# A graph attention kernel: later x groups transposed between the matmuls of v, and the order of its prologue

## The reference

```python
h = jnp.maximum(_layernorm(x, axis=-1), 0.0)          # x: (4096, 256), eps 1e-5
q = h @ Wq.T + bq;  k = h @ Wk.T + bk;  v = h @ Wv.T + bv
a = q @ k.T / sqrt(256) + adj + adj                   # adj: (4096, 4096), added twice
out = x + jax.nn.softmax(a, axis=-1) @ v
```

## Time and profile before

| | before |
|---|---|
| time, median of 3 runs | 810.15 us (810.07 to 2887.47) |
| time of the profiled execution | 809.79 us |
| its span | 808.0 us |
| TensorE busy | 799.6 us, 99% |
| DVE busy | 561.3 us, 69% |
| GpSimd busy | 412.7 us, 51% |
| ACT busy | 357.2 us, 44% |

### The profile page before, as it was taken

The page is one execution under the profiler, slowest core; times in us unless marked ns, Lnnn a source line. Parts: engine busy times, 40 slices in busy tenths (PEclk is TensorE's granted clock), DMA queues, the critical chain, the costliest instruction groups (busy, mean ns, idle before and its releaser), DMA issues.

```text
span 808.0 us, 16606 instructions
## 1 busy us (share of the span) xinstructions
PE 799.6 (99%) x6652; PEld 797.6 (99%) x6652; DVE 561.3 (69%) x942; ACT 357.2 (44%) x637; POOL 412.7 (51%) x377
## 2 busy tenths in 40 slices
PE   9999999999999999999999999999999999999998
PEld 8999999999999999999999999999999999999998
DVE  6868767676676767667677666767766676776754
ACT  5684434434443443444344444344444444443365
POOL 4545719073471917447091643709164380926573
PEclk9999999999999999999999999999999999999999
DMA  8520434333333334333333333423333343333300
GB/s 256 180 94 5 161 91 120 98 112 97 97 114 93 112 98 110 100 98 119 92 111 93 112 105 91 123 92 106 101 111 106 83 123 91 110 105 94 91 27 14
DMA packets 46398, 83.57 MB, mean 103 GB/s; under 512 B 5616, under 2 KB 8304, under 8 KB 46320
## 3 DMA queue, kind: packets, MB, share of 16 engines
q1 hardware_dynamic: 45744, 81.71, 33.5%
q10 hardware_dynamic: 576, 0.79, 0.3%
HBM read 78.25 MB, written 4.23 MB: 102 GB/s over the span
## 4 chain that ended last, share of the span: by engine, by line
PE 95%; DVE 1%; ACT 1%; POOL 1%; issue 1%; DMA 0%; SPq 0%; POOLq 0%; DVEq 0%
PE ps L393 48%; PE ps L495 15%; PE ps L496 15%; PE ps L497 15%; PE ps L385 1%; PE ps L374 1%; DMA ring_b<-in_adj 0%; ACT x_pair L573 0%; PE ps L404 0%; POOL v L329 0%; DVE x_third L680 0%; POOL rstd L315 0%; SPq L234 0%; DVE ring_b L703 0%; ACT v_full L593 0%
## 5 line engine op out<-in xcount | busy, mean ns | idle before, releaser
L393 PE MATMUL ps<-qhl,hT 128*128 128x256 f32 x3072 | 407.2, 282 | 0.6 <-DVE ring_b L703 0.6
L393 PEld LDWEIGHTS ps<-qhl,hT 128*128 128x128 f32 x3072 | 383.9, 190 | 0.8 <-DVE ring_b L703 0.8
L495 PE MATMUL ps<-v,p_hi 128*128 128x258 f32 x1024 | 290.0, 283 | 0.3 <-DVE p_lo L744 0.3
L496 PE MATMUL ps<-v,p_lo 128*128 128x258 f32 x1024 | 288.8, 282 | 0.0
L497 PE MATMUL ps<-v,p_hi 128*128 128x256 f32 x1024 | 288.4, 282 | 0.0
L640 ACT CAST p_hi<-ps 128x512 fp32r<-128x512 f32 x256 | 150.3, 587 | 264.4 <-PE ps L497 262.6
L364 POOL TENSOR_TENSOR ring_a<-ring_a,m_row 128x512 f32<-128x512 f32 x179 | 226.0, 1300 | 16.3 <-ACT m_row L646 15.6
L703 DVE TENSOR_TENSOR ring_a<-ps,ring_a 128x512 f32<-128x512 f32 x179 | 123.3, 689 | 117.3 <-PE ps L393 116.4
L495 PEld LDWEIGHTS ps<-v,p_hi 128*128 128x128 f32 x1024 | 194.7, 190 | 0.5 <-DVE p_lo L744 0.5
L496 PEld LDWEIGHTS ps<-v,p_lo 128*128 128x128 f32 x1024 | 193.8, 189 | 0.0
L497 PEld LDWEIGHTS ps<-v,p_hi 128*128 128x128 f32 x1024 | 193.2, 189 | 0.0
(11 more groups left out here) (82 smaller groups left out, 340.0 us busy)
## 6 DMA issues: line engine op xcount, KB each, us to landing
ring_a<-in_adj SPq DMA_DIRECT2D x179, 256.0 KB, 2.7
ring_b<-in_adj SPq DMA_DIRECT2D x77, 256.0 KB, 2.7
x_res<-in_x SPq DMA_DIRECT2D x16, 256.0 KB, 3.0
out<-x_res SPq DMA_DIRECT2D x15, 256.0 KB, 2.0
x_pair<-in_x SPq DMA_DIRECT2D x5, 512.0 KB, 4.2
term_row<-term_spill SPq DMA_DIRECT2D x14, 128.0 KB, 3.2
x_third<-in_x SPq DMA_DIRECT2D x2, 512.0 KB, 4.3
w_all<-in_w ACTq DMA_DIRECT2D x3, 256.0 KB, 4.3
```

Source lines behind the costliest of these rows:

```text
L393: last = nc.tensor.matmul(dst, lhs(a, ib), rhs(c, ib), start=(n == 0), stop=(n == 3 * DB - 1))
L495: nc.tensor.matmul(ps[:, at, 0:VW], hi, v[:, n, 0:VW], start=(n == 0), stop=False)
L496: nc.tensor.matmul(ps[:, at, 0:VW], lo, v[:, n, 0:VW], start=False, stop=False)
```

## The change

TensorE's iteration of group g, for g from 1 to 6, no longer begins with the 8 transposes of group g + 1. A new function issues v's first half of group g, 12 matmuls, and puts one transpose behind each of the matmuls 3 to 10 (counted from 0), so that four matmuls stand ahead of the first transpose; the waits for the normalized rows and for the free PSUM banks stand between matmul 3 and the first transpose. It is one stream: transposes write to two banks of their own, and the sums of v run on between them. Block 1's q is computed in the last group, directly behind v's first half and ahead of scores(14); the wait for its low part before v's second half is gone, and the next that asks for it is scores(16). The order of ACT's, GpSimd's and SP's lists is unchanged but for `q_hi(1)`, which follows `Q1_GROUP` to group 7. On DVE the statistics of group g + 3 and their aggregation now stand directly behind `add_adj(2g - 1)`, both ahead of `h_lo`, and `h_lo` ahead of `running_max(2g - 1)`; `q_lo(1)` follows to group 7.

```diff
--- before.py
+++ after.py
@@ -24,7 +24,7 @@
     LAG = UNITS + 6
     HOLD = (STEPS - 5,)
     WARM = 20
-    Q1_GROUP = 3
+    Q1_GROUP = GROUPS - 1
     SPLIT_PARTS = 4
     PARTS = GROUPS + 1
     XB = 3
@@ -447,6 +447,27 @@
                                          lambda c, ib: wv_T[:, c, ib, :])
                 last.then_inc(s_vmm, 1)
 
+            def project_v_and_transpose_h(g):
+                pe.wait_ge(s_vhi, 2 * (g - 1) + 1)
+                for n in range(2):
+                    t = GT * g + n
+                    for i, (ib, a, c) in enumerate((ib, a, c) for ib in range(DB) for a, c in ((0, 0), (1, 0), (0, 1))):
+                        m = 3 * DB * n + i
+                        last = nc.tensor.matmul(ps[:, v_bank(g, 0) + n, 0:VW], hT[:, a, ib, t * P:(t + 1) * P],
+                                                wv_T[:, c, ib, :], start=(i == 0), stop=(i == 3 * DB - 1))
+                        if m == 3:
+                            if g + 2 < SPLIT_PARTS:
+                                pe.wait_ge(s_norm2, g + 2)
+                            pe.wait_ge(s_norm, g + 2)
+                            pe.wait_ge(s_hlo, g + 2)
+                        if 3 <= m < 3 + DB * GT:
+                            jb, j = (m - 3) // GT, (m - 3) % GT
+                            turned = nc.tensor.transpose(ps[:, HT_BANK + jb, j * P:(j + 1) * P],
+                                                         rows(g + 1)[:, j, jb * P:(jb + 1) * P], ident[:, :])
+                            if j == GT - 1:
+                                turned.then_inc(s_ht, 1)
+                last.then_inc(s_vmm, 1)
+
             def scores(s):
                 b, u = s // UNITS, s % UNITS
                 if u == 0:
@@ -516,18 +537,16 @@
             project_v(0, 1)
             scores(1)
             for g in range(1, GROUPS):
+                pe.wait_ge(s_hlo, g + 2)
                 if g + 1 < GROUPS:
-                    transpose_h(g + 2)
-                pe.wait_ge(s_hlo, g + 2)
-                project_v(g, 0)
-                scores(2 * g)
+                    project_v_and_transpose_h(g)
+                else:
+                    project_v(g, 0)
                 if g == Q1_GROUP:
                     pe.wait_ge(s_vhi, 2 * g)
                     project_q(1)
-                    scores(2 * g + 1)
-                    pe.wait_ge(s_qlo, 2)
-                    project_v(g, 1)
-                elif g + 1 < GROUPS:
+                scores(2 * g)
+                if g + 1 < GROUPS:
                     project_v(g, 1)
                     scores(2 * g + 1)
             scores(FIRST - 1)
@@ -803,15 +822,14 @@
                 tile_stats(3, j)
             part_stats(4)
             for g in range(1, GROUPS):
-                if g + 1 < GROUPS:
-                    h_lo(g + 2)
                 add_adj(2 * g - 1)
                 if g + XB < GROUPS:
                     for j in range(GT):
                         tile_stats(g + XB, j)
+                    part_stats(g + XB + 1)
+                if g + 1 < GROUPS:
+                    h_lo(g + 2)
                 running_max(2 * g - 1)
-                if g + XB < GROUPS:
-                    part_stats(g + XB + 1)
                 if g == Q1_GROUP:
                     q_lo(1)
                 add_adj(2 * g)
```

## The result

| | before | after |
|---|---|---|
| time, median of 22 runs each | 810.08 us | 808.41 us |
| ratio of the times | | 0.9983, 95% interval 0.9977 to 0.9989 |
| time and span of the profiled execution | 809.79, 808.0 us | 807.8, 806.0 us |
| scores(1)'s first matmul to the turn of block 0's maxima | 53.02 us | 51.50 us |

The change gives 1.67 us, 0.2% (by the interval 0.9 to 1.9 us); 808.5 us was forecast.

What follows compares the result with a forecast made beforehand. TensorE, 99% busy, bounds the kernel, with 3.2 us of lost time at most to recover. Terms of -0.48, -0.69, -0.59 and +0.1 us give -1.65 us: 808.5 us forecast, own range 807.9 to 809.1 us, overall 807.3 to 810.8 us.

Steps and rivals of the forecast that it cites:

- The sum: Whole change: -0.48 - 0.69 - 0.59 = -1.76 us, and +0.1 us for alternation, gives -1.65 us.
- the turn: Sign of being right: the turn of the maxima comes 1.6 to 1.8 us sooner than 71.38 us.
- Wait for x group 2: Group 1: v's first four matmuls fill part of TensorE's wait for DVE's normalization, -0.48 us.
- q's wait: Group 3: moving block 1's q to the last group removes the wait for its low part, -0.69 us.
- the 0.3 us of spare time: Last group: unit 14's logits are added 3.99 us from q's start; scores(16) needs them at 4.3 us.
- The chain behind group 3: Two groups behind group 3: a late start, hardly won back, goes with q's move; 0.64 us less 0.05 us.
- Alternation: Six groups, 48 transposes between matmuls: cost 0 to 0.2 us, taken as +0.1 us.
- the uncovered loads: Rival: weight loads uncovered at each switch between transpose and matmul, 8.2 us less 1.7 us gained, 816.6 us; chance 7%.
- the cheaper matmuls: Rival: a matmul beside a transpose is 0.01 us cheaper, 0.5 us in all, 808.0 us; chance 9%.
- What becomes later: Within groups: ACT's high part of h at 2.39 us, low part 3.45 us, normalizations end 6.6 to 6.7 us; covered.
- The statistics ahead of the low part of h: DVE's list: the move uses time DVE waited for ACT; without it adds are late, not TensorE; 0 us either way.
- The clock: Rival: thinned matmuls lower TensorE's clock to 1.2 GHz, groups 1 to 6 take twice 39.7 us, 849 us; chance 1%.

Runs made afterwards that it cites:

- e1_q_last: Kernel before with only block 1's q moved to the last group, transposes in blocks and DVE's order kept: 808.28 us, 0.9981 of before.
- e3_q_stays: Changed kernel with block 1's q put back into group 3 behind scores(6), with its wait: 808.86 us, 0.9987 of before.
- e11: Kernel before with DVE's new order alone, statistics and aggregation ahead of the low part of h: 809.59 us, 0.9994 of before.
- e4_block_behind_four: Changed kernel with a group's eight transposes in one block behind v's fourth matmul, without alternation: 808.00 us, 0.9978 of before.
- e5b_old_dve_order: Changed kernel with DVE's order of before (low part of h, add, statistics), second series: 809.93 us, 0.9995 of before.
- e8: Changed kernel with both halves of v ahead of eight transposes, ACT and DVE lists adapted, and two adj loads ahead of SP's second spill: 810.04 us, 1.0003 of before.
- e9: Changed kernel, v's halves ahead of transposes, adj loads ahead of second spill, low part of h before DVE's maximum and statistics in groups 1-2: 806.02 us, 0.9950 of before.
- e6: Changed kernel with both halves of v (24 matmuls) ahead of a block of eight transposes, ACT and DVE lists adapted: 810.27 us, 1.0007 of before.
- e7: Changed kernel with the last two adj buffers' first loads ahead of the second spill of score terms on SP: 807.05 us, 0.9966 of before.
- e2: Kernel before with block 1's q still in group 3 but ahead of scores(6): 809.54 us, 0.9997 of before.
- e5: Changed kernel with DVE's order of before (low part of h, add, statistics), first series: 809.97 us, 1.0002 of before.
- e10: Changed kernel, adj loads ahead of SP's second spill, v's first half ahead of eight transposes, DVE's statistics last in the group: 806.42 us, 0.9957 of before.

## Why the prediction was right

The sum was -1.65 us; the medians give -1.67 us and the stretch -1.52 us. That the first two agree to 0.02 us is luck: the interval reaches from 0.9 to 1.9 us, and the turn came 2.0 us sooner, outside the 1.6 to 1.8 us forecast, because 0.48 us of it lie ahead of the change. The mechanism is borne out by the traces, term by term, from the starts of matmuls:

- *Wait for x group 2:* 0.48 us forecast, 0.39 us found (from the last matmul ahead to the first transpose 2.03 us before, 1.64 us after). DVE's normalization ended 0.1 us later against scores(1) than before, having taken 2.41 us instead of 2.33 us.
- *q's wait:* 0.69 us, all of it, shown by e1_q_last. q's low part was written 3.4 us and the add behind it 3.97 us from q's start (62.19 to 66.16 us), 3.99 us having been forecast: the 0.3 us of spare time were real.
- *The chain behind group 3:* 0.59 us, gone. The step named moving q as what removes it, and e1_q_last shows that this is enough. But the rest of the change removes it as well (e3_q_stays), which the prediction said only of slack in general and did not weigh, and 0.35 us of it go with DVE's new order alone (e11). Its reason was only half read: in the second group it was not a late start that is hardly won back, but one GpSimd operation that took 0.74 us in place of 0.20 us beside DVE's running maximum.
- *Alternation:* 0.1 us taken from 0 to 0.2 us; the groups are 0.025 us longer, 0.16 us in all, of which e4_block_behind_four gives the alternation 0.02 us per group. Both the uncovered loads and the cheaper matmuls are refuted. So is the estimate that the prediction drew from the Trainium skill (TensorE: Matmul & The Clock Gate, Back-to-back issue gap), a gain of 0.5 us. That section of the Trainium skill puts a matmul with its weight load above the formula for 128 columns, as the prediction has it, but below it for 512; the pair of transpose and matmul, at 0.232 us, has no such gain in it.
- *What becomes later:* the high part of h starts 2.42 us into the group (49.88 - 47.46) for 2.39 us forecast, the low part 3.48 us for 3.45 us; the normalizations end at 6.5 us for 6.6 to 6.7 us.
- *The statistics ahead of the low part of h:* priced at nothing, "0 us either way". This step was wrong. It said that without the move the adds would be late, "not TensorE", and stopped there; scores(2g+1) waits for that add at 5.2 us into the group, and DVE ends it at 5.3 us. e5b_old_dve_order shows 0.25 us per group, 1.5 us together. Against the kernel before the move takes 0.36 us off the stretch (e11; 0.9994 in time, not clear of noise), but without it the later low part of h would have taken back the whole gain. It was the condition of the change and not a neutral part; the sum came out all the same, since the change contains it.
- *The clock:* 1.00 in every group shown. The row of the first twenty transposes, which the prediction took for the price of the lower level, does not show that level: the trace of before gives the granted clock as 1.00 there too.

## What to carry to other kernels

A late operation on one engine is paid again by the groups behind it when the chain that it feeds is only just shorter than the period; an edit that ends it is not to be added to one that gives the chain more time, since they have the same term. When a producer is made later, list every consumer engine's order behind it: the work queued behind the blocked instruction (here an add of other data) can be what stops the critical engine, and the list of waits may not show it, while distances between starts do. Where the order on a nearly full engine is changed, reordering the second engine decides: the same edit on TensorE gave 1.0003 and 0.9950 of the time with two orders on DVE (e8 and e9; 1.5 us of the 4.2 us between their stretches were the lower clock behind e8's wait, below). And look at the length of small operations on the chain: one that is longer in one group than in the others points at what runs beside it.

## What the runs showed of the hardware

- A transpose and a matmul that alternate take 0.232 us together, 0.0025 to 0.004 us more than in blocks (0.109 and 0.120 us). Weight loads stay covered in both directions: an uncovered one showed as 0.11 us.
- DVE's running maximum between SBUF tensors took 0.69 us by itself and 1.66 to 1.71 us when it began beside GpSimd's subtraction of v (30.73 and 30.78 us in the rows of e8_both): it ended 0.5 us behind GpSimd. The other way round, GpSimd's operation of 0.20 us took 0.74 us when it began 0.01 us behind DVE's running maximum (54.58 and 54.59 us in the rows of before), and ended 0.06 us behind it. DVE's adds, which read PSUM, kept their 0.68 us beside GpSimd's subtraction (32.49 and 32.52 us in the rows of e5b). The Trainium skill (SBUF — State Buffer, SBUF: two separate sides) has it that the two engines share one pair of ports, which an operation keeps to its end, and that a DVE operation with two SBUF inputs has to wait for a GpSimd one that reads SBUF; the trace agrees.
- A wait in the prologue can cost more than its length. Behind the 2.66 us wait of e8_both the granted clock was at its lower level (0.50, 1.2 GHz) for about 3.4 us (0.70 over 1.7 us, 0.50 over 2 us, 0.90 over 2 us), and v's 24 matmuls took 4.50 us to the next transposes where they take 2.98 us in e6: 1.5 us on top.

```profile
33.00:35.30 2.30, 0.00 (x0) 0.00 (x0) 2.27 (x9) 0.97 (x3) 1.44 (x3) 1.00 0.52 198
35.30:37.00 1.70, 1.63 (x10) 1.63 (x10) 1.67 (x4) 0.00 (x0) 0.67 (x3) 0.70 0.00 0
37.00:39.00 2.00, 2.00 (x11) 2.00 (x11) 1.97 (x6) 1.12 (x3) 0.00 (x0) 0.50 0.00 0
39.00:41.00 2.00, 2.00 (x18) 2.00 (x18) 0.70 (x5) 0.18 (x2) 1.19 (x1) 0.90 0.00 0
```

  (Length, busy us by engine, PEclk, DMA share, GB/s.) It need not: behind the wait of 2.2 us at the same place in e6 the clock stayed at 1.00. Six of the 22 executions of the changed kernel have a mean clock of 0.997 or 0.998 over the run and took 809.3 to 809.8 us, the rest 807.8 to 808.7 us. What lowers it in those six isn't shown, since only the profiled execution has a trace. e6's profiled execution has a mean of 0.998 too, and there the clock was at its lower level from about 11.8 to 15 us, ahead of everything that the change touches; scores(1) began at 19.75 us, 1.9 us later than in the changed kernel. The gap at x group 2 is not shown to be a cause: e9, which has none, has 1.000 in all five executions, but so have e1, e3, e5b, e7 and e11, which have it, in all their 46 (e2, e4, e5 and e10 have one or two lower ones each).
